# Order of work in three layer norms of a two-layer MetaFormer kernel: where variances, spreads and reciprocals stand, and how many units are scaled in a turn

## The reference

```python
x = x + L0_conv(_ln_c(x))          # norm 0, then four sweeps over rows and columns
t = to_tokens(x)
t = t + L0_ffn(_ln_t(t))           # norm 1, then routing, pooling, experts
x = from_tokens(t)
x = x + L1_conv(_ln_c(x))          # norm 2, then four sweeps
t = to_tokens(x)
t = t + L1_ffn(_ln_t(t))           # norm 3, projection, batch norm, a recurrence of 3600 steps
# _ln: (v - mean) / sqrt(var + eps) over the 64 channels
```

## Time and profile before

| | us |
|---|---|
| median of 3 runs | 4235.26 (4232.78 to 4238.69) |
| profiled execution, own time | 4230.19 |
| its span, first to last instruction | 4228.4 |
| PE / ACT / DVE busy in the span | 4126.6 / 2062.3 / 1328.9 |

### The profile page before, as it was taken

The page is one execution under the profiler, slowest core; times in us unless marked ns, Lnnn a source line. Parts: engine busy times, 40 slices in busy tenths (PEclk is TensorE's granted clock), DMA queues, the critical chain, the costliest instruction groups (busy, mean ns, idle before and its releaser), DMA issues.

```text
span 4228.4 us, 138285 instructions
## 1 busy us (share of the span) xinstructions
PE 4126.6 (98%) x57200; PEld 3129.7 (74%) x57200; DVE 1328.9 (31%) x2576; ACT 2062.3 (49%) x8972; POOL 119.9 (3%) x243
## 2 busy tenths in 40 slices
PE   8999999998889999999998899999999999999999
PEld 3999999994442999999993466666666666666666
DVE  4655433334546655533335600000000000000000
ACT  6002344435545002344444366666666666666666
POOL 1000000000010000000000000000000000000000
PEclk9999999999999999999999899999999999999999
DMA  6000000004258000000007200000000000000000
GB/s 158 1 0 0 0 0 0 0 0 141 71 137 254 7 0 0 0 0 0 0 0 200 73 22 15 22 19 18 22 16 22 22 16 22 15 22 22 16 22 19
DMA packets 178469, 144.93 MB, mean 34 GB/s; under 512 B 110910, under 2 KB 177502, under 8 KB 178014
## 3 DMA queue, kind: packets, MB, share of 16 engines
q1 hardware_dynamic: 177486, 137.58, 12.4%
q10 hardware_dynamic: 528, 0.63, 0.1%
HBM read 79.19 MB, written 58.98 MB: 33 GB/s over the span
## 4 chain that ended last, share of the span: by engine, by line
PE 94%; DVE 2%; ACT 1%; issue 1%; SPq 1%; DMA 1%; POOL 0%; DVEq 0%; ACTq 0%; POOLq 0%
PE ps L977 24%; PE ps L827 22%; PE ps L798 18%; PE ps L896 16%; PE ps L891 3%; PE ps L600 2%; PE ps L635 1%; PE ps L594 1%; PE ps L611 1%; PE ps L768 1%; PE ps L621 1%; PE ps L868 1%; PE ps L666 1%; SPq L405 1%; PE ps L749 0%
## 5 line engine op out<-in xcount | busy, mean ns | idle before, releaser
L977 PE MATMUL ps<-xl,vt 65*32 65x8 f32 x28800 | 1693.3, 187 | 0.0
L1189 ACT ACTIVATE xl<-ps 64x8 f32<-64x8 f32 x7200 | 1224.0, 170 | 595.4 <-PE ps L977 1.5
L896 PE MATMUL ps<-idle 128*32 128x256 bf16 (+1 forms) x5828 | 1496.4, 271 | 3.6 <-POOL ident L514 3.6
L977 PEld LDWEIGHTS ps<-xl,vt 65*32 65x32 f32 x28800 | 1037.4, 108 | 622.1 <-ACT xl L1189 0.2
L827 PE MATMUL ps<-xl,taps 128*128 128x128 f32 (+2 forms) x7880 | 912.4, 279 | 4.7 <-DVE xl L1410 4.7
L827 PEld LDWEIGHTS ps<-xl,taps 128*128 128x128 f32 x7880 | 912.0, 191 | 5.4 <-issue 5.3
L798 PEld LDWEIGHTS ps<-split 128*128 128x128 f32 x4140 | 773.8, 189 | 10.7 <-issue 9.3
L798 PE MATMUL ps<-split 128*128 128x400 f32 x4140 | 780.6, 351 | 0.0
L1498 DVE TENSOR_TENSOR xl<-xl 64x320 f32<-64x320 f32 x180 | 125.2, 696 | 1695.2 <-ACT xl L1189 1695.2
L1044 ACT ACTIVATE img<-xl 128x144 f32 x788 | 366.8, 466 | 546.5 <-DVE xl L1400 546.5
L896 PEld LDWEIGHTS ps<-idle 128*32 128x32 bf16 x5828 | 577.5, 99 | 13.9 <-issue 3.6
(11 more groups left out here) (154 smaller groups left out, 1666.0 us busy)
## 6 DMA issues: line engine op xcount, KB each, us to landing
ring<-in_x_dram SPq DMA_DIRECT2D x144, 200.0 KB, 3.7
x_dram<-sums SPq DMA_DIRECT2D x144, 200.0 KB, 3.3
t_dram<-sums SPq DMA_DIRECT2D x72, 200.0 KB, 3.6
ring<-t_dram SPq DMA_DIRECT2D x72, 200.0 KB, 3.8
ring<-x_dram SPq DMA_DIRECT2D x72, 200.0 KB, 3.7
xl<-x_dram SPq DMA_DIRECT2D x45, 320.0 KB, 5.2
out_dram<-xl SPq DMA_DIRECT2D x45, 320.0 KB, 3.5
img<-in_L_ffn_weight_dram SPq DMA_DIRECT2D x4, 512.0 KB
```

Source lines behind the costliest of these rows:

```text
L896: pe.matmul(PS[bank][0:32, 0:n], idle[:, 0:32], idle[:, 0:n], start=True, stop=True)
L977: last = pe.matmul(PS[2 * s + h][c * 32:(c + 1) * 32, t * HB:(t + 1) * HB], vt[:, c * 32:(c + 1) * 32], prev, start=False, stop=True, skip ...
L1189: act.activation(yb[0:64, s, h * HB:(h + 1) * HB, t], PS[2 * s + h][0:64, t * HB:(t + 1) * HB], ACT.Sigmoid).then_inc(step_y[h], 1)
```

## The change

**Norm 0, PE.** The spreads of two units move from the front of an odd turn to its end, behind the mean.

**Norms 0 and 2, DVE.** In the two turns of a group's reciprocals these stand ahead of the scaling, not behind it; `low_taps` goes from turn 22 to turn 27.

**Norm 3.** Groups end at 10, 18, 26, 32 and 36 (five groups, so one more square root and four more reciprocal parts). A table `TOKEN_TURN` says which units are spread and scaled in which turn: two in turns 13, 17, 29, 32 and 35 to 37, 39 and 40, none in 38, one otherwise. So 28 units instead of 22 are scaled by turn 35, and the last at turn 40 instead of 49. The four parts of the reciprocal stand together in turns 12, 20, 28, 34 and 38, right behind the total. The seven-bank tail begins with unit 28. Norm 1 keeps its instructions (its spread function only gets a name of its own).

```diff
-        GROUP = {0: NCH + 1, 1: NCH, 2: NCH + 1, 3: NCH}
+        GROUP_ENDS = {0: (10, 20, 30, UNITS), 1: (9, 18, 27, UNITS), 2: (10, 20, 30, UNITS), 3: (10, 18, 26, 32, UNITS)}
+        TOKEN_TURN = {n: list(range(a, b)) for n, a, b in zip(range(13, 42), (0, 2, 3, 4, 5, 7, 8, 9, *range(10, 18), 18, 20, 21, 22, 24, 25, 26, 28, 30, 32, 32, 34),
+                                                              (2, 3, 4, 5, 7, 8, 9, 10, *range(11, 19), 20, 21, 22, 24, 25, 26, 28, 30, 32, 32, 34, UNITS))}
+        TOKEN_TAIL = 28
...
+            def spread_out(n):
+                if n == TOKEN_TAIL:
+                    pe.wait_ge(st.kept, 2 * UNITS)
+                pe.wait_ge(st.inverse, INVERSES * (place_of(i, n)[0] + 1))
+                for v in range(2):
+                    j = 2 * n + v
+                    if j - 2 * TOKEN_TAIL >= len(TOKENS_LAST):
+                        pe.wait_ge(st.normed, j - len(TOKENS_LAST) + 1)
+                    elif j >= 2:
+                        pe.wait_ge(st.normed, min(j - 1, 2 * TOKEN_TAIL))
                     spread_one(pe, i, n, v, token_spread_bank(i, n, v))
...
-            for n in range(UNITS + LAG):
-                if LAG <= n:
-                    spread_out(n - LAG)
+            for n in range(max(TOKEN_TURN) + 1):
+                for m in TOKEN_TURN.get(n, []):
+                    spread_out(m)
                 if n + 1 < UNITS:
                     move(n + 1)
...
             for n in range(UNITS + 1):
-                if LAG <= n < UNITS and (i == 2 or n % 2):
-                    for p in range(n - LAG - (i == 0), n - LAG + 1):
-                        spread_out(p)
+                if i == 2 and LAG <= n < UNITS:
+                    spread_out(n - LAG)
...
                 if 0 < n <= UNITS:
                     variances(pe, i, n - 1, row_squares)
+                if i == 0 and LAG <= n < UNITS and n % 2:
+                    for p in (n - LAG - 1, n - LAG):
+                        spread_out(p)
...
-                if n >= 2 and (n - 2) % NCH == NCH - 1:
-                    take_std(act, i, (n - 2) // NCH)
+                if n - 1 in GROUP_ENDS[i]:
+                    take_std(act, i, GROUP_ENDS[i].index(n - 1))
...
+            scaled = []
+            for n in range(max(TOKEN_TURN) + 2):
                 if n < UNITS:
                     total(n)
-                if m >= 0:
+                if n - 2 in GROUP_ENDS[i]:
+                    for part in range(INVERSES):
+                        invert(dve, i, GROUP_ENDS[i].index(n - 2), part)
+                for m in scaled:
                     bn_take(dve, m, 0)
-                if LAG <= n < UNITS + LAG:
-                    scale(n - LAG)
-                if m >= 0:
+                for m in TOKEN_TURN.get(n, []):
+                    scale(m)
+                for m in scaled:
                     bn_take(dve, m, 1)
-                if NCH <= n < UNITS + NCH and 2 <= n % NCH < 4:
-                    for part in range(INVERSES // 2):
-                        invert(dve, i, n // NCH - 1, (n % NCH - 2) * INVERSES // 2 + part)
+                scaled = TOKEN_TURN.get(n, [])
...
+                for since in (3, 4):
+                    if n - since + 1 in GROUP_ENDS[i]:
+                        for part in range(INVERSES // 2):
+                            invert(dve, i, GROUP_ENDS[i].index(n - since + 1), (since - 3) * INVERSES // 2 + part)
                 if n >= LAG:
                     for h in range(2):
                         scale_row(dve, i, n - LAG, h)
...
-                elif n == LAG + 8:
+                elif n == LAG + 13:
                     low_taps(dve, i // 2)
```

More of the change, by code:

```diff
@@ L288, in metaformer @@
         INVERSES = 4
-        GROUP = {0: NCH + 1, 1: NCH, 2: NCH + 1, 3: NCH}
+        GROUP_ENDS = {0: (10, 20, 30, UNITS), 1: (9, 18, 27, UNITS), 2: (10, 20, 30, UNITS), 3: (10, 18, 26, 32, UNITS)}
+        TOKEN_TURN = {n: list(range(a, b)) for n, a, b in zip(range(13, 42), (0, 2, 3, 4, 5, 7, 8, 9, *range(10, 18), 18, 20, 21, 22, 24, 25, 26, 28, 30, 32, 32, 34),
+                                                              (2, 3, 4, 5, 7, 8, 9, 10, *range(11, 19), 20, 21, 22, 24, 25, 26, 28, 30, 32, 32, 34, UNITS))}
+        assert sum(TOKEN_TURN.values(), []) == list(range(UNITS))
+        TOKEN_TAIL = 28
         IN_NORM = UNITS - LAG
@@ L300, in place_of @@
         def place_of(i, n):
-            return n // GROUP[i], n % GROUP[i]
+            g = sum(n >= end for end in GROUP_ENDS[i])
+            return g, n - (GROUP_ENDS[i][g - 1] if g else 0)
         def group_end(i, g):
-            return min(GROUP[i] * (g + 1), UNITS)
+            return GROUP_ENDS[i][g]
         def row_spread_bank(i, p, h):
@@ L346, in token_spread_bank @@
                 return ROUTE_SPREAD[j % len(ROUTE_SPREAD)]
-            return SPREAD32[v] if n < LAST else TOKENS_LAST[(j - 2 * LAST) % len(TOKENS_LAST)]
+            return SPREAD32[v] if n < TOKEN_TAIL else TOKENS_LAST[(j - 2 * TOKEN_TAIL) % len(TOKENS_LAST)]
         def by_rows(t, hp):
@@ L582, in variances @@
             st, (g, k) = ln[i], place_of(i, n)
-            size = group_end(i, g) - g * GROUP[i]
+            size = group_end(i, g) - (n - k)
             if k % 2 == 0 and k < size - 1:
@@ L637, in centre_and_project, with spread_routed @@
                 last.then_inc(st.centred, 1)
-            def spread_out(n):
+            def spread_routed(n):
                 g, k = n // NCH, n % NCH
-                banks = ROUTE_SPREAD if i == 1 else TOKENS_LAST if n >= LAST else SPREAD32
-                since = 2 * NCH * g if i == 1 else 2 * LAST if n >= LAST else 0
                 if k == 0:
-                    if i == 1 or n == LAST:
-                        pe.wait_ge(st.kept, 2 * (n + NCH))
-                    if i == 1:
-                        for _ in range(14):
-                            keep_clock(pe, 512, MOVE[1])
+                    pe.wait_ge(st.kept, 2 * (n + NCH))
+                    for _ in range(14):
+                        keep_clock(pe, 512, MOVE[1])
                     pe.wait_ge(st.inverse, INVERSES * (g + 1))
@@ L651, in spread_out @@
                     j = 2 * n + v
-                    if j - since >= len(banks):
-                        pe.wait_ge(st.normed, j - len(banks) + 1)
-                    elif j >= 2 and i == 3:
-                        pe.wait_ge(st.normed, min(j - 1, 2 * LAST))
+                    if j - 2 * NCH * g >= len(ROUTE_SPREAD):
+                        pe.wait_ge(st.normed, j - len(ROUTE_SPREAD) + 1)
+                    spread_one(pe, i, n, v, token_spread_bank(i, n, v))
+            def spread_out(n):
[8 more added lines that the diff above has]
+                        pe.wait_ge(st.normed, min(j - 1, 2 * TOKEN_TAIL))
                     spread_one(pe, i, n, v, token_spread_bank(i, n, v))
@@ L685, in pe_token_norm @@
                         if n < first + NCH:
-                            spread_out(n)
+                            spread_routed(n)
                         if n > first:
@@ L1308, in dve_row_norm @@
                         scale_row(dve, i, n - LAG, h)
-                for since in (3, 4):
-                    g = place_of(i, n - since)[0]
-                    if n >= since and n - since + 1 == group_end(i, g):
-                        for part in range(INVERSES // 2):
-                            invert(dve, i, g, (since - 3) * INVERSES // 2 + part)
                 if n == LAG + 6:
                     line_ends(dve, i // 2)
-                elif n == LAG + 8:
+                elif n == LAG + 13:
                     low_taps(dve, i // 2)
```

2 lines of the change are left out of this document (removed).

## The result

The changed kernel is slower: median 4244.19 us against 4232.34 us for the kernel before (19 runs each), ratio 1.0027 with a 95% interval of 1.0021 to 1.0034. That is 11.9 us more where 5.4 less were forecast, and above the range of 4214 to 4240.

| stage, profiled executions | before, us | after, us | difference |
|---|---|---|---|
| norm 0, first spread to first sweep | 55.45 | 42.46 | -13.0 |
| norm 2, first mix to first sweep | 114.2 | 114.2 | 0.0 |
| norm 3, first move to aggregate | 170.8 | 195.1 | +24.3 |
| all the rest | | | -2.2 |

What follows compares the result with a forecast made beforehand. PE and ACT, coupled by their order, bound norm 0; PE paces norm 3, DVE its tail. Norm 0 -13.3, norm 2 -0.6 and norm 3 +8.5 sum to -5.4 us: 4229.8 us, range 4214 to 4240.

Steps and rivals of the forecast that it cites:

- 13.3 us less: Norm 0, first spread to first sweep: 55.45 us was to become 42.2.
- the bank loop: Norm 0: an odd unit's second half needs the bank of the even unit's first half; 3.62 us a period against 4.47.
- the end: End of norm 0: mean, spread to DVE, four scales and the first line, 4.2 us.
- the rival of the loads: Norm 0: loads set a period of 4.0 us, so 9.5 us less there and 4233.7 in all; chance 10%.
- The reciprocals cost nothing: Norm 0: reciprocals ahead of the scaling end at about 7.6 us, before the first spread needing them at 8.1.
- 0.6 less forecast: Norm 2: DVE's new order and half of a possible clock gain, between 2.5 less and 1.3 more.
- 0.7 slower at equal clock: Norm 2 without the 1.25 us of clock gain: 0.6 earlier at the second group, 1.3 later afterwards.
- forecast 18.1: Norm 3's main part: two-unit turns and early reciprocals make total 35 end 18.1 us later.
- forecast 26.6: Norm 3's tail: 23.4 us of DVE work plus waits of 0.6 and 2.6, 9.6 us less than before.
- a two-unit turn at 2.1 us: Norm 3: the second unit waits for the same two banks, so the move comes at 2.95 us instead of 0.88.
- The rival of half clock: Norm 3: clock falls in turn 29 and stays down through turns 30 to 35, 19.8 us more, 4249.7; chance 8%.
- The rival in which norm 3 gains (25%): Norm 3: DVE's 0.91 us of slack a turn swallows the waits, 4.3 us less, 4217 in all; chance 25%.

Runs made afterwards that it cites:

- norms02_only: Changed kernel with norm 3 put back to that of the kernel before; 4218.14 us against 4233.49, ratio 0.9962.
- filler_wide: Changed kernel plus idle bf16 matmuls, 128 columns of weights, ahead of and between the spreads of the two-unit turns; 4233.19 us, ratio 0.9999.
- pe_order_only: Kernel before with only PE's order in norm 0 changed, DVE's order and norm 3 as before; 4227.76 us against 4233.52, ratio 0.9986.
- move_between: Changed kernel with the next unit's move put between the two units' spreads in norm 3; 4233.03 us, ratio 1.0000.
- one_unit_turns: Changed kernel with one unit per turn in norm 3, thirteen turns behind its total, uneven groups and early reciprocals kept; 4228.60 us against 4233.49, ratio 0.9989.
- early_nine: norms02_only with norm 3's lag thirteen instead of fourteen and its four reciprocal parts at once ahead of the scaling; 4226.18 us against 4232.05, ratio 0.9987.
- both last fillers: filler_wide, and the same kernel with 32 instead of 128 columns of weights in its idle matmuls; 4233.19 and 4229.43 us.

## Why the prediction was wrong

**Norm 0: right in the main, and so close by luck.** 13.3 us less were forecast, 13.0 came. The periods of 3.65 fit the bank loop's 3.62; no run tests that loop apart from the others. But the ten periods with what ACT adds to them were counted as 38.0 us and took 39.05, 1.0 of it in waits for loads, and the end was counted as 4.2 and took 3.4. With the same code the other traces gave 10.8 to 12.7 less. So the rival of the loads, with 9.5 less, is partly borne out: PE waited 1.0 us for loads in this norm 0, 2.3 in that of norms02_only, 2.8 in that of filler_wide. The reciprocals cost nothing, as argued, because DVE's edit hides them: without it (pe_order_only) they take 5.2 us.

**Norm 2: small, as said.** 0.6 less forecast, 0.0 measured, with 6.8 us at half clock before and 3.4 after. At full clock the new order looks 1.6 us slower: 41.30 + 70.40 us in parts of two profiles with the old order, 41.47 + 71.82 in move_between, none of them with half clock. The forecast had 0.7 slower at equal clock.

**Norm 3: the terms held, the clock did not.** With the clock held in the two-unit turns (filler_wide, at the same clock at the norm's start), total 35 ends 21.1 us late, forecast 18.1, 1.3 of it at the half clock behind turn 20; the tail takes 27.9, forecast 26.6. In the changed kernel the same figures are 31.2 and 29.3. So the step that failed is the one that sized a two-unit turn at 2.1 us: it counted the move at 2.95 us instead of 0.88, which the trace of the changed kernel confirms, and left out what the clock does behind it. Turn 13 against one_unit_turns cost 6.5 us by total 16, turn 17 the same by total 20, turn 29 some 6 by total 31; turn 32, at full clock, about 3. With the clock held by the wide filler the four cost 2.4 to 3.0 us each, so the 2.1 was a little small by itself. On that count the three turns with the half clock behind them make 12.7 of the 13.1 us by which the main part was missed (31.2 against 18.1). In turn 35 the half clock makes PE's last centring late, and DVE waits 1.37 and 4.88 us in the tail where 0.6 and 2.6 were counted: 3.1 us more, against the 2.7 by which the tail was missed.

**Norm 3 in parts**, from the table above: the shorter lag -0.7 (168.1 to 167.4), early four-part reciprocals +9.4 (to 176.8), uneven groups +3.4 (to 180.2), two units in a turn +0.7 with the clock held (to 180.9; 11.9 in the main part and 11.2 back in the tail), half clock behind them +11.5 (to 192.4). The sum is 24.3. These are steps from one kernel to the next, and the half clock is in more than the last: early_nine's step holds some 5.5 us of it that one_unit_turns doesn't have, so that by estimate the early reciprocals are 3.9 and the uneven groups 8.9, with a tail at half clock in it. With the clock held in the two-unit turns, two units in a turn bring nothing either: the tail gives back what the waits take.

**The rival of half clock** named the right mechanism and was given 8%. Its place was wrong: it put the fall behind the early reciprocals, one fall that stays, where it came behind turns with two units, three times for 10.2 us and then for the tail. The prediction argued that no row of norm 3 showed a fall at waits of this length. True of the rows, but the trace of the kernel before had falls behind short waits: in norm 2, the first row, behind a single wait of 1.28 us,

```profile
1327.77 1.37 PE L749 MATMUL ps<-img,gate_lhg 32*64 32x400 f32 x8 [1.28 <-DVE sums L1300]
```

and in norm 3's first turns, the 6.8 us at half clock that no row shows, behind waits of 1.47 and 0.73 us. And a change that puts two waits and two spreads into one turn makes exactly what no row of norm 3 had. The Trainium skill (TensorE: Matmul & The Clock Gate, A second HAM failure mode: psum-queue depth-cycling) tells of a kernel in which short idle times of PE between groups of matmuls, as it cycled through PSUM banks, made the clock go up and down. By that rule the two-unit turns, with their waits for banks, were suspect; the trace agrees in part: in turns 13 and 17 PE was never idle for longer than 0.92 us, and 10.2 us at half clock followed each, but in move_between's turn 13 they followed without any wait for a bank.

**The rival in which norm 3 gains (25%)** is out: DVE's slack of 0.91 us a turn didn't swallow the waits even with the clock held.

## What to carry to other kernels

When an edit gathers short waits of PE in one turn, price the half clock that may follow, not the waits alone: here a turn that was to cost 2.1 us cost 6.5, because 10.2 us at half clock followed. A reciprocal belongs as early as the square root ahead of it is done when DVE gets there, and not earlier: in norm 0 the early place met that and saved 5.2 us of waits, in norm 3 it didn't and cost some 4 us at full clock (by estimate), 9.4 with the half clock. And one trace is one sample: ten traces of the same norm 0 differ by 2.2 us.

## What the runs showed of the hardware

The granted clock fell to half although PE had been busy for most of the time around it: in move_between's turn 13 PE's longest idle time near the fall was 0.92 us, with two units' spreads behind it, whose weights are 32 rows by 128 columns (32*128 in the rows). The same 0.92 us with one spread behind it (one_unit_turns) left the clock full. Idle bf16 matmuls, 0.6 to 1.25 us at a time in the waits of the turn, kept it full in turns 13, 17 and 29, with 32 columns of weights as with 128; in turn 32 it fell with the narrow ones. The same code can go either way: norm 3's first turns, which are the same in all thirteen traces, had 6.8 us at half clock in five of them and none in eight. What exactly in such a turn decides isn't settled by these runs: the fall behind turn 20 came in early_nine (10.2 us) and in both last fillers (3.4), and not in the changed kernel, though DVE's 2.02 us of standing still are the same in all of them.
